# Second attention: two short causal blocks of scores share a PSUM bank and one read

## What is computed

```
q = _heads(x @ Wq + bq);  k = ...;  v = ...            # 16 heads of 16
att = jnp.einsum('bhqd,bhkd->bhqk', q, k) * scale
att = jnp.where(causal[None, None], att, -jnp.inf)     # the causal part
y = jnp.einsum('bhqk,bhkd->bhqd', jax.nn.softmax(att, axis=-1), v)
qc = _heads(x @ Wcq + bcq);  kc, vc = from the context, 512 long
attc = jnp.einsum('bhqd,bhkd->bhqk', qc, kc) * scale   # the cross part, not masked
y = y + jnp.einsum('bhqk,bhkd->bhqd', jax.nn.softmax(attc, axis=-1), vc)
return y.transpose(0, 2, 1, 3).reshape(x.shape[0], T, C) @ Wp + bp
```

## Time and profile before

| | us |
|---|---|
| median of 3 runs | 1284.3 |
| lowest, highest | 1284.05, 1286.31 |
| the profiled execution | 1287.09 |
| its span, first to last instruction | 1285.4 |
| second attention in it | about 577 to 1021 |

### The profile page before, as it was taken

How to read it: one execution, slowest core, us unless ns; L and a number is a source line. 1 busy time by engine, 2 the same in 40 slices (tenths; PEclk the granted TensorE clock), 3 DMA queues, 4 the chain that set the end, 5 groups by cost and what they waited for, 6 DMA issues and landing times.

```text
span 1285.4 us, 25128 instructions
## 1 busy us (share of the span) xinstructions
PE 1183.4 (92%) x8870; PEld 542.9 (42%) x8870; DVE 924.5 (72%) x2376; ACT 820.9 (64%) x1577; POOL 498.6 (39%) x519
## 2 busy tenths in 40 slices
PE   6799999999999999868899988888888999999998
PEld 2344444444444444334333233322332366666666
DVE  3777777777777777767788787778876567656564
ACT  3566666666666666634677766676666777667663
POOL 0167878888777778914212111131111131000000
PEclk9999999999999999988999999999999899999999
DMA  7634333322233332021121221122100523232300
GB/s 221 172 98 117 96 93 84 111 80 80 80 84 83 84 82 81 13 71 42 46 81 43 65 61 42 43 56 69 42 26 1 197 89 109 75 139 97 118 17 17
DMA packets 82483, 103.00 MB, mean 80 GB/s; under 512 B 12627, under 2 KB 74067, under 8 KB 82327
## 3 DMA queue, kind: packets, MB, share of 16 engines
q1 hardware_dynamic: 81174, 100.87, 26.8%
q10 hardware_dynamic: 160, 0.39, 0.1%
q0 software_dynamic: 1024, 0.13, 0.1%
HBM read 65.37 MB, written 10.68 MB: 59 GB/s over the span
## 4 chain that ended last, share of the span: by engine, by line
PE 75%; DVE 14%; ACT 4%; issue 4%; DMA 1%; POOL 1%; ACTq 0%; SPq 0%; DVEq 0%; POOLq 0%
PE a_s L1299 10%; PE a_o L464 9%; DVE a_mx L1607 8%; PE a_m L1285 7%; PE a_o L1218 6%; PE a_a L409 6%; PE a_s L454 5%; PE a_s L455 4%; PE a_m L1173 4%; PE a_e L504 3%; PE a_a L419 3%; PE a_m L432 3%; PE a_a L166 3%; PE a_s L1200 3%; PE a_s L1285 2%
## 5 line engine op out<-in xcount | busy, mean ns | idle before, releaser
L1607 DVE TENSOR_REDUCE a_mx<-a_m 128x1 f32<-128x512 f32 (+3 forms) x512 | 271.5, 583 | 80.4 <-PE a_m L1173 71.3
L1432 ACT ACTIVATE a_pt<-a_s 128x512 f32<-128x512 f32 (+3 forms) x512 | 235.0, 515 | 115.4 <-PE a_s L1200 112.9
L635 ACT ACTIVATE a_pt<-a_s 128x512 f32<-128x512 f32 x256 | 149.5, 597 | 167.4 <-DVE a_s L762 139.6
L753 DVE CUSTOM_DVE_ANT_0 a_junk<-a_m,a_rtile 128x512 f16<-128x512 f32 x256 | 167.3, 687 | 0.7 <-issue 0.7
L844 POOL TENSOR_TENSOR a_ps<-a_ps,a_pt 128x512 f32<-128x512 f32 x128 | 159.8, 1271 | 0.7 <-ACT a_pt L635 0.7
L464 PE MATMUL a_o<-a_pt,a_v 128*64 128x512 f32 x512 | 139.8, 624 | 2.6 <-DVE a_a L767 2.5
L1853 POOL TENSOR_SCALAR_AFFINE_SELECT a_pt<-a_pt 128x512 f32<-128x512 f32 x64 | 40.6, 635 | 229.4 <-ACT a_pt L1432 229.4
L762 DVE TENSOR_TENSOR a_s<-a_s,a_near 128x218 f32<-128x218 f32 (+1 forms) x256 | 107.9, 433 | 13.8 <-PE a_s L455 10.6
L454 PE MATMUL a_s<-a_q,a_k 128*128 128x512 f16 x256 | 99.3, 388 | 7.1 <-ACT a_pt L635 6.1
L742 DVE TENSOR_TENSOR a_nat<-a_a,a_nat 128x512 f16<-128x512 f32 x64 | 44.3, 692 | 84.2 <-ACT a_nat L610 84.2
L844 POOL TENSOR_TENSOR a_ps<-a_pt 128x512 f32<-128x512 f32 x64 | 80.1, 1273 | 57.0 <-ACT a_pt L635 57.0
(11 more groups left out here) (295 smaller groups left out, 2622.8 us busy)
## 6 DMA issues: line engine op xcount, KB each, us to landing
a_rtile<-lines SPq DMA_DIRECT2D x32, 448.0 KB, 3.9
a_q<-a_nat SPq DMA_DIRECT2D x192, 64.0 KB
a_k<-a_nat SPq DMA_DIRECT2D x192, 64.0 KB
a_vy<-in_Wa SPq DMA_DIRECT2D x12, 1024.0 KB, 4.9
a_vy<-in_Wb SPq DMA_DIRECT2D x12, 1024.0 KB, 7.4
a_qk<-halves SPq DMA_DIRECT2D x40, 128.0 KB, 2.7
halves<-a_held SPq DMA_DIRECT2D x16, 256.0 KB, 2.3
halves<-a_held SPq DMA_DIRECT2D x32, 128.0 KB, 2.4
```

Source lines behind the costliest of these rows:

```text
L635: act.activation(pt[:, n % RING, ::-1], bank_s[j % 2][:, :], ACT.Exp, scale=SC1 / QS).then_inc(sm["act_s"], 1)
L753: dve.tensor_tensor_reduce(junk[h][:, :], bank_m[h][:, :], rtile[:, u % 3, h, qb * P:qb * P + S], 1.0, -3e38, ALU.add, ALU.max, mx[u % 2][ ...
L1432: act.activation(pt[g % 4][:, h, first:], bank_s[(32 * u + j) % 3][:, first:], ACT.Exp, scale=SC2 / QS).then_inc(sm["act_s"], 1)
L1607: dve.tensor_reduce(mx[u % 2][:, qb, to:to + 1], bank_m[j % 3][:, 0:keys], AX.X, ALU.max).then_inc(sm["dve_b"], 1)
```

## The change

Where two causal tiles of the same `h` fit into one bank, they share it. For the maxima this is `qb` = 0 and 1 (tiles of 128 and 256 columns): the heads `h` of pair 0 and of pair 1 lie side by side in one bank, and one DVE instruction reduces the two, with two results per partition. Both pairs are done at steps 0 and 4; steps 2 and 6 have no maxima. For the scores it is `kb` = 2 and 3 (256 and 128 columns): both pairs at steps 10 and 12, one ACT instruction over two heads, no scores at steps 11 and 13. A unit then has 28 maxima tiles and 28 score tiles instead of 32 and 32; the semaphores count in these numbers. The number of matmuls, of columns and of all other instructions is unchanged.

```
+        def max_pairs(i):
+
+            x, qb, pair = max_group(i)
+            if x == 0 and qb < 2:
+                return (0, 1) if pair == 0 else ()
+            return (pair,)
+
+        MAX_TILES = [(i, h) for i in range(SLOT) for h in range(2) if max_pairs(i)]
+        TILES_M = len(MAX_TILES)
+
+        def score_tiles(i):
+
+            x, kb, h = i // 8, i // 2 % NT, i % 2 * 2
+            if x == 0 and kb > 1:
+                return ((0, 2), (1, 3)) if h == 0 else ()
+            return ((h,), (h + 1,))
+
+        TILES_S = sum(len(score_tiles(i)) for i in range(SLOT))
+
+        def scores_at(u, i):
+
+            return TILES_S * u + sum(len(score_tiles(k)) for k in range(i))
+
...
-                x, qb, pair = max_group(i)
-                keys, mm = (qb + 1) * P if x == 0 else S, [None, None]
+                x, qb, _ = max_group(i)
+                keys, pairs, mm = (qb + 1) * P if x == 0 else S, max_pairs(i), [None, None]
                 if i == 0:
                     pe.wait_ge(sm["moved"], MOVES * DMA * (u + 1))
                 if i == 0 and u == 0:
                     pe.wait_ge(sm["cst"], 3 * DMA)
-                for h in range(2):
-                    j, o = 32 * u + 2 * i + h, h * FAR
-                    if j > 2:
-                        pe.wait_ge(sm["dve_b"], j - 2)
-                    mm[h] = pe.matmul(bank_m[j % 3][:, 0:keys], q[u % 3][o:o + ROW_M, pair, x, qb * P:(qb + 1) * P],
-                                      k[u % 3][o:o + ROW_M, pair, x, 0:keys], start=True, stop=x == 1)
-                if x == 0:
-                    for n in range(2):
-                        for h in range(2):
-                            j, o = 32 * u + 2 * i + h, h * FAR
-                            mm[h] = pe.matmul(bank_m[j % 3][:, qb * P:(qb + 1) * P], identm[o:o + FAR, n, :],
-                                              tri_q[o:o + FAR, n, :], start=False, stop=n == 1)
-                for h in range(2):
-                    mm[h].then_inc(sm["pe_b"], 1)
+                for a, pair in enumerate(pairs):
+                    for h in range(2):
+                        j, o = TILES_M * u + MAX_TILES.index((i, h)), h * FAR
+                        if j > 2 and a == 0:
+                            pe.wait_ge(sm["dve_b"], j - 2)
+                        mm[h] = pe.matmul(bank_m[j % 3][:, a * keys:(a + 1) * keys], q[u % 3][o:o + ROW_M, pair, x, qb * P:(qb + 1) * P],
+                                          k[u % 3][o:o + ROW_M, pair, x, 0:keys], start=True, stop=x == 1)
+                    if x == 0:
+                        for n in range(2):
+                            for h in range(2):
+                                j, o, at = TILES_M * u + MAX_TILES.index((i, h)), h * FAR, a * keys + qb * P
+                                mm[h] = pe.matmul(bank_m[j % 3][:, at:at + P], identm[o:o + FAR, n, :],
+                                                  tri_q[o:o + FAR, n, :], start=False, stop=n == 1)
+                if pairs:
+                    for h in range(2):
+                        mm[h].then_inc(sm["pe_b"], 1)
 
...
-            def score(u, j):
-                x, kb, h = j // 16, j // G2 % NT, j % G2
-                o, first = h % 2 * FAR, kb * P if x == 0 else 0
-                if j == 0:
+            def score(u, i):
+                x, kb = i // 8, i // 2 % NT
+                first, tiles = kb * P if x == 0 else 0, score_tiles(i)
+                if i == 0:
                     pe.wait_ge(sm["row"], 2 * DMA * (u + 1))
-                if 32 * u + j > 2:
-                    pe.wait_ge(sm["act_s"], 32 * u + j - 2)
-                else:
-                    pe.wait_ge(sm["act_f"], FILLS)
-                pe.matmul(bank_s[(32 * u + j) % 3][:, first:], k[u % 3][o:o + ROWS, h // 2, x, kb * P:(kb + 1) * P],
-                          q[u % 3][o:o + ROWS, h // 2, x, first:], start=True, stop=True).then_inc(sm["pe_s"], 1)
+                for a in range(len(tiles[0]) if tiles else 0):
+                    for m, heads in enumerate(tiles):
+                        n, o = scores_at(u, i) + m, heads[a] % 2 * FAR
+                        if a == 0 and n > 2:
+                            pe.wait_ge(sm["act_s"], n - 2)
+                        elif a == 0:
+                            pe.wait_ge(sm["act_f"], FILLS)
+                        mm = pe.matmul(bank_s[n % 3][:, a * (S - first):(a + 1) * (S - first)],
+                                       k[u % 3][o:o + ROWS, heads[a] // 2, x, kb * P:(kb + 1) * P],
+                                       q[u % 3][o:o + ROWS, heads[a] // 2, x, first:], start=True, stop=True)
+                        if a == len(heads) - 1:
+                            mm.then_inc(sm["pe_s"], 1)
 
...
-                    score(u, 2 * i)
-                    score(u, 2 * i + 1)
+                    score(u, i)
...
-            def exponential(u, j):
-                x, kb, h = j // 16, j // G2 % NT, j % G2
-                first, g = kb * P if x == 0 else 0, j // G2
-                if j % G2 == 0 and 8 * u + g > 3:
+            def exponential(u, i, m):
+                x, kb, heads = i // 8, i // 2 % NT, score_tiles(i)[m]
+                first, g, n = kb * P if x == 0 else 0, i // 2, scores_at(u, i) + m
+                if i % 2 == 0 and m == 0 and 8 * u + g > 3:
                     act.wait_ge(sm["pe_o"], 8 * u + g - 3)
-                act.wait_ge(sm["pe_s"], 32 * u + j + 1)
-                act.activation(pt[g % 4][:, h, first:], bank_s[(32 * u + j) % 3][:, first:], ACT.Exp, scale=SC2 / QS
-                               ).then_inc(sm["act_s"], 1)
+                act.wait_ge(sm["pe_s"], n + 1)
+                to = pt[g % 4][:, heads[0]:heads[-1] + 1:2, first:]
+                act.activation(to, bank_s[n % 3][:, 0:len(heads) * (S - first)].rearrange("p (a s) -> p a s", a=len(heads)), ACT.Exp,
+                               scale=SC2 / QS).then_inc(sm["act_s"], 1)
 
...
-                x, qb, pair = max_group(i)
-                keys = (qb + 1) * P if x == 0 else S
+                x, qb, _ = max_group(i)
+                keys, pairs = (qb + 1) * P if x == 0 else S, max_pairs(i)
                 if i == 0 and u > 1:
                     dve.wait_ge(sm["dve_n"], u - 1)
-                for h in range(2):
-                    j, to = 32 * u + 2 * i + h, h * G2 + pair * 2 + x
+                for h in range(2 if pairs else 0):
+                    j, to = TILES_M * u + MAX_TILES.index((i, h)), h * G2 + pairs[0] * 2 + x
                     dve.wait_ge(sm["pe_b"], j + 1)
-                    dve.tensor_reduce(mx[u % 2][:, qb, to:to + 1], bank_m[j % 3][:, 0:keys], AX.X, ALU.max
+                    dve.tensor_reduce(mx[u % 2][:, qb, to:to + 2 * len(pairs) - 1:2],
+                                      bank_m[j % 3][:, 0:len(pairs) * keys].rearrange("p (a s) -> p a s", a=len(pairs)), AX.X, ALU.max
                                       ).then_inc(sm["dve_b"], 1)
 
```

More of the change, by code:

```diff
@@ L1065, in sync @@
                 if u >= 3:
-                    sp.wait_ge(sm["pe_s"], 32 * (u - 3) + 32)
+                    sp.wait_ge(sm["pe_s"], TILES_S * (u - 2))
                 if u == 1:
@@ L1213, in pv @@
                 else:
[L1214 removed]
+                    pe.wait_ge(sm["act_s"], scores_at(u, 2 * g + 2))
                 if kb == 0 and 2 * u + x > 0:
@@ L1279, in upward @@
                 if (u, f) == (0, 3):
-                    pe.wait_ge(sm["act_s"], 32 * UNITS)
+                    pe.wait_ge(sm["act_s"], TILES_S * UNITS)
                 if FT * u + f > 3:
@@ L1482, in split @@
                     elif u == 1:
-                        act.wait_ge(sm["pe_s"], 32 * (UNITS - 1))
+                        act.wait_ge(sm["pe_s"], TILES_S * (UNITS - 1))
                     else:
@@ L1492, in gelu @@
                 if u == 0 and f == 0:
-                    act.wait_ge(sm["pe_s"], 32 * UNITS)
+                    act.wait_ge(sm["pe_s"], TILES_S * UNITS)
                 if FT * u + f > 3:
@@ L1512, in scalar @@
                 if u is not None:
-                    exponential(u, 2 * i)
-                    exponential(u, 2 * i + 1)
+                    for m in range(len(score_tiles(i))):
+                        exponential(u, i, m)
                 if 0 <= n - FILL < FILLS:
```

7 lines of the change are left out of this document (3 added, 4 removed).

## The result

| | before | after |
|---|---|---|
| median, us (11 runs each, in turn) | 1284.12 | 1289.22 |
| lowest, highest | 1278.9, 1289.25 | 1288.03, 1294.67 |
| ratio of after to before, 95% interval | | 1.005, 1.003 to 1.007 |
| profiled execution, its span | 1287.09, 1285.4 | 1288.03, 1286.3 |
| its mean granted clock | 0.981 | 0.980 |

The change makes the kernel 5.1 us slower; the forecast was 1.9. The profiled executions lie only 0.9 us apart: that of after was the fastest of its runs, with a clock of 0.980, where six of the eleven had 0.976 or 0.977 and four 0.974. This is the first trace of the cause.

The account below looks back on a forecast made before the run. TensorE, DVE and ACT were taken as nearly full, each waiting in turn, the chain through TensorE in steps 1 to 8. 11 x 0.22 - 0.5 = +1.9 us on 1284.3 gave 1286.2 us, range 1280.5 to 1289.5.

Parts of the forecast that it names:

- The merged instructions: DVE and ACT: each costs what one of its size costs, 418 and 683 ns on DVE, 383 and 594 on ACT.
- Rival 4: A merged instruction costs as much as the two, 562 instead of 418 ns at step 0: 1287.7 us, chance 0.07.
- Steps 0 to 2: DVE's longer first reduction costs 0.14 us; step 2's saving turns into waiting for ACT: +0.10 us a unit (0 to +0.14).
- a few hundredths: Steps 1 and 2: ACT's first exponential comes later by the delay of step 1's maxima, less this slack in us.
- Step 4: Step 6's pair of maxima moves ahead of step 4's scores, projection and `pv`: +0.22 us a unit (0.11 to 0.32).
- Steps 5 and 6: With step 6's maxima gone a wait shortens, ACT's exponential coming last: -0.13 to -0.18 us, copy 0 to -0.06, mean -0.10.
- A unit: Sum of the terms for one unit, 0.10 + 0.22 - 0.10 = +0.22 us, counted for eleven units.
- Rivals 1 and 2: First: DVE or ACT bounds throughout, 1274.8 us, chance 0.09. Second: ACT's ring does not hold, 1274 us, chance 0.08.
- rival 3: Merged groups only push back and step 6 returns nothing: 0.46 us in each of 14 units, 1290.7 us, chance 0.08.
- The last unit: Scores without maxima: TensorE's waits for ACT at steps 11 and 12 go, -0.5 us, once.
- I price them at nothing: Units before and after the eleven between 657 and 906 us: the change was taken to cost or gain nothing there.
- the half case of rival 1: Half of the DVE or ACT saving of 0.59 us a unit arrives: 1279.5 us.

Follow-up runs that it names:

- qb0_only: The changed kernel with the maxima merged only for query block 0, scores still merged: 1292.0 us, ratio 1.005.
- qb1_only: The changed kernel with the maxima merged only for query block 1 (both pairs in step 4), scores still merged: 1291.4 us, ratio 1.005.
- copy_first: The kernel before with ACT's copy L1449 moved ahead of the exponentials of its step, nothing merged: 1285.0 us, ratio 1.000.
- refill_after: The changed kernel with the first product of the maxima made twice in steps 9, 11, 13 and 15: 1294.0 us, ratio 1.009.
- refill_before: The kernel before with the first product of the maxima made twice in steps 9, 11, 13 and 15: 1298.0 us, ratio 1.011.
- early_qb1: The changed kernel with query block 1's merged maxima at step 2, none at 4 and 6: 1282.1 us, ratio 0.998.

## Why the prediction was wrong

- **The merged instructions** cost what was forecast, to 4 ns. Rival 4 is out.
- **Steps 0 to 2, +0.10**: measured +0.16 in the unit shown and +0.16 in `qb0_only`. Of the right kind and too small: the two score tiles of step 2 took the whole saving back, and the slack of "a few hundredths" was not there.
- **Step 4, +0.22**: the rows show 0.11 + 0.11.
- **Steps 5 and 6, -0.10**: the mechanism held, ACT's exponential comes last there. The sizes were the wrong way about: -0.09 without the copy (1.62 us instead of 1.71; -0.13 to -0.18 forecast) and -0.28 with it (0 to -0.06 forecast). `qb1_only` has steps 4 to 6 together at +0.12, which is 0.22 - 0.10.
- **A unit, +0.22**: +0.27 (0.15 to 0.35). Over units 2 to 9 that is 2.2 us, where the forecast would have had 1.8. Rivals 1 and 2 are out, and so is the mechanism of rival 3 (0.46 us a unit), though its 1290.7 lies near the time, by luck.
- **The last unit, -0.5**: from the mark of unit 15 to the `pv` behind the last merged scores (1008.23 in before, 1009.17 in after) the profiles read 19.6 us before and 21.6 after. Taking off the 1.8 us of the eight slow products and the 0.6 of a slow `pv` leaves 19.2, a gain of some 0.4, about what was forecast; an estimate.
- **"The units before it are filled by projections of the whole input, those after it run at the lower clock or with more work of the last steps; I price them at nothing"**: this is the step that failed, twice. The smaller part is a real gain: the copy L1449 came free (0.5 us in unit 13, 0.85 by `copy_first`). The larger part is that the sum has no term for the clock: the forecast took the time at half clock as given, the same before and after. It is not a property of the place. With a delay of some 0.2 us per unit, which the forecast had nearly right in size, mean H was 14.5 us higher, and that was worth 5.0 us, more than all its terms together.
- **The range.** 1289.2 lies just inside the stated 1280.5 to 1289.5, and that is luck: the bounds came from the forecast's terms and the rivals, and none of them was the clock. The lower bound calls 1280.5 the half case of rival 1, for which the prediction has 1279.5 elsewhere.
- **On the median.** I put the sum on the median of before and did not ask why three runs of one kernel differed by 2.3 us. By the line above such a spread is the clock's for the most part (these three have no clock on record), and it was the row to read.

What stays open: by what rule a shift raises or lowers H. Shifts of +0.12 to +0.27 us per unit had 54 to 75 us, those of 0.00 to 0.08 had 40 to 57; but `refill_after`, with +0.87, had 44 us and the change 59, and more merging had less H than half of it. The Trainium skill's page "TensorE: Matmul & The Clock Gate" says, in its section "A second HAM failure mode: psum-queue depth-cycling", that short idle times between groups of matmuls, as the banks are cycled, can make the clock fall and rise again. The traces agree as far as that goes: in the 7 us ahead of each fall in units 1 to 15, in all 18 profiles, TensorE idled several times and never for more than 1.96 us at a time. But if short idle times were all, more work should hold the clock, and `refill_before` has more work and the lower clock; and the place at 799.3 and 800.6 us, with the same busy times, lost the clock in one execution of two. Where in time such a place falls seems to count too, which would let a small shift act either way; no run tests that.

## What to carry to other kernels

Before costing an edit in tenths of a microsecond, plot the time of single runs over the mean granted clock: where it explains the spread, an edit's effect on the clock is a term of its own, with both signs, and belongs into the range and among the rivals. To tell it from the edit, run a control that adds the same delay without the edit. A merged read saves only if the place to which its producer's work moves is one where that producer waits: block 1's pair cost 0.12 us a unit at step 4 and nothing, even a little less, at step 2, where TensorE waited for ACT. Of this change the half to keep is the merged scores: 0.997 (0.995 to 0.998 and 0.995 to 0.999) in two sets, the fastest version tried, with `early_qb1` 0.4 us behind it.

## What the runs showed of the hardware

- One program on one core ran at mean clocks from 0.974 to 0.990 in separate executions, 1278.5 to 1293.5 us: 0.34 us of time for each us at half clock.
- A stretch at half clock lasted 3.4 to 24 us. At half clock eight products took 3.71 us instead of 1.92, and eight of the `pv` 1.60 instead of 0.98.
- Work that was the same in two executions of one kernel, with TensorE busy 3.79 and 3.80 of 5.00 us, was followed by a fall of the clock in one and not in the other.
- A reduction to two results per partition costs DVE no more than one to a single result (414 and 685 ns against 418 and 683), and two pieces in the output cost ACT nothing (381 against 383).
- Behind another reduction, the same 128-wide reduction added 0.20 us to the chain, though its row says 0.28 (676.54 to 677.03, 0.49 us, where 0.29 stood): in DVE's timeline it is recorded from 676.74, 0.08 us before the end of the one ahead of it.
